# A 64-expert layer with three of four batches sorted, its indexed reads moved inside the causal attention

## The reference, cut to what matters

```python
# sub-layer 8 ("L2_ffn"): 64 experts, each token takes the best 8
scores = softmax(x @ gate_w.T)
topk_w, topk_ids = top_k(scores, 8);  topk_w /= topk_w.sum(-1) + 1e-20
h = silu(rows @ w_gate[e].T) * (rows @ w_up[e].T)      # 96 wide, per expert e
y = sum over the 8 of topk_w * (h @ w_down[e].T)
# sub-layer 9 ("L3_attn"): causal attention, 16 heads of 8, then a layer norm
att = where(causal, q @ k.T / sqrt(8), -inf);  y = layernorm(softmax(att) @ v @ Wo + bo)
```

## Time and profile before

| what | us |
|---|---|
| median of 3 runs | 1896.92 |
| lowest and highest of them | 1888.32, 1905.2 |
| the profiled execution | 1892.54 |
| its span, first to last instruction | 1890.8 |
| mean granted TensorE clock | 0.946 |

### The profile page before, as it was taken

How to read it: one execution, slowest core, us unless ns; L and a number is a source line. 1 busy time by engine, 2 the same in 40 slices (tenths; PEclk the granted TensorE clock), 3 DMA queues, 4 the chain that set the end, 5 groups by cost and what they waited for, 6 DMA issues and landing times. The chain is left out here.

```text
span 1890.8 us, 50187 instructions
## 1 busy us (share of the span) xinstructions
PE 1677.6 (89%) x19970; PEld 1202.2 (64%) x19970; DVE 1131.9 (60%) x2410; ACT 977.4 (52%) x2317; POOL 706.1 (37%) x947
## 2 busy tenths in 40 slices
PE   7883899775799999999999878899999999999885
PEld 4332899343457889989888753567996655454332
DVE  5534445559556777877776434676657866555334
ACT  4651444548586666666674435234553253445562
POOL 1103311305256777666775201473006621223101
PEclk9996999886699999999999989899999999999998
DMA  7401786000031000000000040523643200000100
GB/s 298 177 1 57 210 241 204 25 1 1 1 145 48 26 15 25 14 15 25 15 24 16 26 201 1 129 78 110 169 135 83 66 5 1 2 2 1 41 1 24
DMA packets 75929, 125.69 MB, mean 66 GB/s; under 512 B 10728, under 2 KB 55152, under 8 KB 74320
## 3 DMA queue, kind: packets, MB, share of 16 engines
q1 hardware_dynamic: 67696, 106.69, 17.5%
q0 software_dynamic: 6912, 15.61, 2.8%
q10 hardware_dynamic: 1088, 0.13, 0.0%
HBM read 83.73 MB, written 38.67 MB: 65 GB/s over the span
## 5 line engine op out<-in xcount | busy, mean ns | idle before, releaser
L2947 DVE SCALAR_TENSOR_TENSOR big<-bank,pack,big 128x256 f32<-128x256 f32 (+2 forms) x384 | 181.4, 474 | 40.6 <-ACT mask L2836 25.4
L2174 ACT ACTIVATE pack<-bank 128x512 f32<-128x512 f32 x96 | 57.5, 600 | 159.6 <-PE bank L834 93.8
L2643 PE MATMUL bank<-y,pack 128*128 128x262 f32 (+1 forms) x384 | 134.5, 435 | 5.5 <-DVE big L2947 5.1
L3375 ACT ACTIVATE pt<-bank 128x1024 f32<-128x1024 f32 (+3 forms) x128 | 84.2, 704 | 105.7 <-PE bank L3221 105.5
L3405 DVE TENSOR_REDUCE part<-bank 128x8 f32<-128x1024 f32 (+1 forms) x80 | 95.6, 1220 | 68.2 <-PE bank L3202 68.2
L2553 POOL TENSOR_TENSOR big<-big,mask 128x256 f32<-128x256 f32 (+1 forms) x128 | 93.7, 732 | 111.2 <-DVE big L2947 110.0
L2835 ACT ACTIVATE big<-bank,pack 128x256 f32<-128x256 f32 x192 | 91.1, 475 | 84.3 <-PE bank L2643 78.8
L1979 POOL DMA_INDIRECT pack<-results,where x64 | 67.0, 1047 | 151.2 <-PE bank L2049 137.6
L832 PE MATMUL bank<-yh,wl 128*128 128x512 f32 x192 | 113.3, 590 | 10.9 <-DVE a L2330 8.3
L2630 PEld LDWEIGHTS bank<-big 128*128 128x128 f32 x896 | 113.3, 193 | 7.1 <-issue 1.4
L2630 PE MATMUL bank<-big 128*128 128x128 f32 x896 | 116.2, 277 | 0.0
(11 more groups left out here) (672 smaller groups left out, 4396.7 us busy)
## 6 DMA issues: line engine op xcount, KB each, us to landing
big<-in_experts SPq DMA_DIRECT2D x46, 516.0 KB
big<-in_big SPq DMA_DIRECT2D x1, 9216.0 KB, 25.9
gate<-big SPq DMA_DIRECT2D x32, 256.0 KB
z<-gate SPq DMA_DIRECT2D x16, 512.0 KB
pack<-routing SPq DMA_DIRECT2D x60, 128.0 KB
wide_sorted<-big SPq DMA_DIRECT2D x5, 1472.0 KB, 13.1
pack<-in_pack SPq DMA_DIRECT2D x1, 5910.5 KB, 21.5
pack<-wide_sorted SPq DMA_DIRECT2D x16, 256.0 KB, 3.2
```

Source lines behind the costliest of these rows:

```text
L2643: nc.tensor.matmul(haloed(i)[:, :, 3 - halo:], k.w["L2_attn_qkv_w"][:, sl(m, P)], tokens, start=True, stop=True).then_inc(s["raw"], 1)
L2947: ins = nc.vector.scalar_tensor_tensor(out=d, in0=conv_in(i, back), scalar=weight(i, 3 - back), in1=d, op0=ALU.mult, op1=ALU.add)
L3375: nc.scalar.activation(dst, src, ACT.Exp, scale=-1.0).then_inc(s["weights"], 1)
```

## The change

Sub-layer 8 now has one dense batch (2) and three sorted ones (3, 0, 1), `WIDE_ORDER` = (2, 3, 0, 1):

- All 48 blocks of the one dense batch run ahead of the tiles; none run behind them. The table of router weights is half as wide; blocks below 3 are split by GpSimd.
- 96 indexed writes in place of 64; they no longer wait for down products. `locate`, `situate`, `code`, `put` work on 768 columns in place of 512. 159 tiles (80 pairs) in place of 127 (64 pairs).
- Behind the dense blocks, ahead of the tiles: batch 2 is added to x, its attention norm, q, k, v, per-head keys and the first 6 of its 20 looks.
- The indexed reads, the sums and the joins leave sub-layer 8. Sub-layer 9 takes the batches in `WIDE_ORDER`. It starts with the 14 remaining looks of batch 2 and 16 of 96 reads; the other 80 reads are dealt out over 36 units (`GATHERS`). ScalarE scales each read row (8 instructions on 128 x 128 for each of 12 tiles), and VectorE sums the 8 with one reduction.
- For each of the three sorted batches the following stands in the units of the batch before it: four tiles scaled and summed, `join`, norm, q, k, v, per-head keys, all 20 looks. The looks therefore come in the last three (batch 0 in the order) or five units.

In `layer6` the last token block's key transposes and their copies are left out, with the waits that this needs.

```diff
-WIDE_TILES = (2 * S * 8 + 64 * (P - 1)) // P
-WIDE_SPLIT, WIDE_POOLED, WIDE_MAP_AT = 24, 6, 13
+K8, WIDE_ORDER = 8, (2, 3, 0, 1)
+WIDE_ROWS = 3 * TB
+WIDE_TILES = (WIDE_ROWS * P * K8 + 64 * (P - 1)) // P
+WIDE_POOLED, WIDE_MAP_AT = 3, 13
...
-            for i in range(HALF):
+            for i in range(ROWS):
                 for c in range(K8):
-                    after(pool, s["down"], (i * K8 + c) * 2 // 3)
-                    nc.gpsimd.indirect_dma_start(out=rows_in, ...
+                    nc.gpsimd.indirect_dma_start(out=rows_in, ...
...
+            pe.wait_ge(s["done"], 1)
+            nc.tensor.matmul(first_xc, k.w["centre"], x[:, sl(DENSE)], start=True, stop=True).then_inc(s["first_centred"], 1)
...
+            for n in range(EARLY_LOOKS):
+                if n == 0:
+                    pe.wait_ge(s["k_out"], 1)
+                after(pe, s["most"], n - 2)
+                look_products(nc, k, late, 0, n, both(n)).then_inc(s["scores"], 1)
...
+            pe.wait_ge(s["v_out"], 1)
+            pe.wait_ge(s["most"], EARLY_LOOKS)
             pe.wait_ge(s["down_in"], 16)
             address(0)
             turn(0)
...
+    GROUPS, UNITS, KEEP, LAG = 4, 16, 4, 3
+    JOIN, QK, V, SHIFT = (9, 7, 7), (12, 10, 10), (13, 11, 11), (14, 13, 13, 13)
+    per_unit = [(0,) * 13 + (6, 7, 7)] + [(0,) * 11 + (4, 4, 4, 5, 3)] * 2
+    HEAD_GATHERS = 16
+    GATHERS = (2,) * 8 + (1,) * 5 + (5,) * 3 + (3, 2, 2, 2, 2, 2) + (1,) * 5 + (4,) * 5 + (2, 2, 1, 1)
...
+            def scale_rows(i):
+                act.wait_ge(s[f"got_{i % TB}"], 16 * K8 * (i // TB + 1))
+                for c in range(K8):
+                    row = found[:, sl(i % TB * K8 + c, P)]
+                    ins = nc.scalar.activation(row, row, ACT.Copy, scale=late.share[:, c * WIDE_ROWS + i:][:, 0:1])
+                ins.then_inc(s["rows_scaled"], 1)
...
+            def mix(i):
+                dve.wait_ge(s["rows_scaled"], i + 1)
+                parts = found[:, sl(i % TB, K8 * P)].rearrange("p (c e) -> p e c", c=K8)
+                nc.vector.tensor_reduce(mixed[:, sl(i % TB, P)], parts, AX.X, ALU.add).then_inc(s["mixed"], 1)
...
-                elif phase == KT:
+                elif phase == KT and u // B < TB - 1:
```

More of the change, by code:

```diff
@@ new lines, with look_products @@
+EARLY_LOOKS, EARLY_ROWS = 6, 2
+def look_products(nc, k, late, b, n, dst):
+    i, kind, key, w, js, gp = LOOKS[n]
+    if kind == 0:
+        for gl in range(2):
+            nc.tensor.matmul(dst[:, sl(gl)], k.ident_bf, late.later4[:, :], start=True, stop=False, skip_group_check=True)
+    for c, j in enumerate(js):
+        for gl in range(2):
+            rows = sl(2 * gp + gl, 32)
+            mm = nc.tensor.matmul(dst[:, gl * S + c * w:][:, 0:w], late.qj[b][rows, j * S + i * P:][:, 0:P], late.kd[b][rows, key:key + w],
+                                  start=kind != 0, stop=True, tile_position=(rows.start, 0), skip_group_check=True)
+    return mm
@@ L1866, in layer8 @@
[L1866 to L1872 removed]
+        whole, number, codes = sb("whole", MOST + 2, I32), sb("number", MOST + 2), sb("codes", K8)
@@ L1931, in _ @@
                 store(p)
-            for q in range(before, G // 4):
-                bring_rep(q)
         @block.gpsimd
@@ L2035, in unit @@
+                pe.wait_ge(s["mapped"], 2)
+                for i in range(2):
+                    mm = nc.tensor.matmul(mapped[0:1, sl(i, P)], expert[:, i:i + 1], k.ident, start=True, stop=True)
+                mm.then_inc(s["mapped_ps"], 1)
+            def unit(m):
                 if m < WIDE_POOLED:
@@ L2394, in _ @@
             strike(1)
-            mark()
-            order()
-            order_kept()
-            for m in range(WIDE_SPLIT):
-                dense(m)
-                if m == 1:
+            mark(1)
+            order(1)
+            for m in range(J):
+                scale(m)
+                hidden(m)
+                if m == 0:
+                    locate()
+                    situate()
+                    code()
+                    put()
+                if WIDE_POOLED <= m + 2 < J:
+                    split_low(m + 2)
+                if m == 2:
```

844 lines of the change are left out of this document (424 added, 420 removed).

## The result

| | before | after |
|---|---|---|
| time, us (median, lowest to highest, 4 runs each) | 1895.86 (1888.32 to 1905.2) | 2066.45 (2063.92 to 2069.39) |
| ratio, 95% interval | | 1.0898 [1.0847, 1.0949] |
| span of the profiled execution, us | 1890.8 | 2064.6 |
| forecast, us | | 1884 (1842 to 1912) |

The account below looks back on a forecast made before the run. TensorE was taken as the bound, busy for 89% of the span. -120.0 + 29.1 + 25.1 + 1.3 + 2.4 - 31.0 + 87.7 - 3.0 = -8.4 took 1892.5 to 1884 us, range 1842 to 1912.

Parts of the forecast that it names:

- Part 2: Way to the first tile: dense blocks at 2.27 us, then a serial chain; first tile at 1336.0, +29.1 us.
- rival C: Dense stage: router loads set the blocks' pace, dense half ends some 20 us later, time 1902; chance 0.13.
- The misread row: Dense stage: a VectorE gap was blamed on router loads behind the 3 MB down-weight load; 6 us taken after the change.
- The chain behind the dense stage: Batch 2 behind its dense blocks, from down product through norm, q, k and looks to the last maximum: 26.5 us.
- Part 3: Tiles: 16 more pairs at 1.57 us each cost +25.1; table load +1.3, last eviction and stage change +2.4.
- Part 4: Attention prologue: 52.0 us go, 14 looks with turn and shift take 21 us beside 16 indexed reads; -31.0.
- Part 5: The 64 attention units: 273.5 us instead of 185.8, paced by GpSimd, ScalarE and serial chains; +87.7.
- Rival B: Attention units: thinly used TensorE lets its clock drop, adding 30 us, time 1914; chance 0.15.
- the serial chain to the keys: Attention units: from `join` through add, norm, q, k and placing to the first look, some 15.3 us per sorted batch.
- Rival A: Attention units: slack and spread reads and copies hide half of 66.9 us; time 1850, 1817 if all hidden; chance 0.27.
- Parts 1 and 6: Second dense half goes, -120.0 us; sub-layer 6 loses 8 groups of key transposes, -3 us.

Follow-up runs that it names:

- experiment 3: Kernel before the change, with only the wait of its 64 indexed writes on the down products taken out: 1947.4 us.
- experiment 5: Changed kernel with a wait put back on the indexed writes, one block per two writes (write n waits for n/2 down products): 1956.1 us.
- Experiment 12: Kernel before the change, with the wait of indexed write n moved from 2n/3 down products to 6 + 5n/8: ratio 0.9988 [0.9962, 1.0014].
- experiment 4: Changed kernel with the 3 MB load of the down weights issued behind all router-row loads: 2063.2 us.
- experiment 1: Changed kernel with the dropped wait put back, two blocks per three writes (write n waits for 2n/3 down products, at most 48): 1980.7 us.
- experiment 6: Kernel of experiment 1 with two bf16 products of 512 columns added ahead of each weigh in units 0 to 12 of each batch: 2044.8 us.
- experiment 7: Kernel of experiment 1 without the 96 indexed reads and the waits on them; scaled copies and sums stay, on stale rows: 1970.4 us.
- experiment 8: Changed kernel, writes still without a wait on TensorE, with four short GpSimd fills behind each indexed write: 1991.5 us.
- experiment 9: Kernel of experiment 5 with added bf16 products in units 9 to 11, six ahead of the normalized rows' wait, twelve ahead of the keys': 1935.85 us.
- experiment 10: Changed kernel with each of the 96 indexed writes as a plain 64 KB transfer, ungated and without fills; attention reads stay indexed: 1942.3 us.
- experiment 11: Changed kernel with one wait for all 48 down products ahead of the first indexed write: 2042.1 us.

## Why the prediction was wrong

**Part 2, the way to the first tile, is the step that failed.** It priced the writes rightly (1.26 us each, 121 us; measured 1.28 and 123) and took the dense blocks beside them at 2.27 us. I listed "ungated writes" as a side note of rival C and gave the lost gate no price of its own, because in before the writes seemed to cost TensorE nothing. Apart from the small gap they cost nothing there because of the gate. The term was +29.1; it came out at +133.4. With a gate of one block per two writes the first tile product stands at 1347.6 instead of 1446.9: 99 of the 104 us over the forecast are the lost wait, shown from both sides by experiments 3 and 5. That the wait does it is shown; how it keeps TensorE's signals on time is open, as experiment 5 contradicts the theory of the unbroken row.

**The misread row.** The gap of before was read as router loads behind a 3 MB transfer. Experiment 12 took the gap away without touching a load, and experiment 4 moved the load without touching the loss. The row even said so: the releaser that it named was another tensor, and I overruled it with a story. Had I looked at what lies beside the gap (17 writes that the gate did not hold), the main loss was there to be read at a scale of 7 us. In the versions that let the blocks run beside the indexed writes (experiments 1 and 5 to 9) a router load does hold VectorE once, for 4.3 to 6.1 us, and the dense stage ends at 1307.9 to 1312.7 us, where I had 1309.5. So those 6 us came true, by a row that did not show them.

**The chain behind the dense stage** was forecast at 26.5 us and takes 31.6 (1408.7 to 1440.3), within its bounds.

**Part 3, the tiles.** 80 pairs from 1446.9 to 1572.9 are 1.575 us each. That looks like the 1.57 of the forecast, but the forecast's figure took in both ends of the stage. By the same borders the 64 pairs of before, from 1311.4 to 1407.7, are 1.505 each. So a pair has become dearer. Eight pairs take 1.84 to 1.94 us where before has 1.32 to 1.41, and TensorE's weight loads wait for VectorE as often (waits of 1460 to 1565 us below; in all the tiles of before the like wait is 0.2 us):

```profile
PEld bank L2125 <- DVE a L2400: 5.0, 8, 0.7
```

Of the 7.0 us over, 4.6 are the pairs (126.0 us against 96.3 + 25.1) and 2.4 the ends of the stage. Why VectorE is later there was not taken apart.

**Part 4, the prologue.** 21 us forecast, 35.2 measured. From the first read to the first cut it takes 38.4 us in the changed kernel and 38.2 and 38.1 in experiments 1 and 4, but 24.5 to 29.0 in experiments 5, 6 and 8 to 11, which have the same 16 reads (the forecast, to the first cut, was 24). Without the reads it is no shorter than in the faster of these: from the last tile product to the first cut experiment 7 takes 28.8 us, experiment 8 with its reads 28.6. The 16 head reads are indexed transfers without a wait on TensorE too, and late signals are in the changed kernel's trace: two maxima start 1.2 and 3.5 us after the modelled end of their look. That they make the difference is only argued; why it strikes in some executions alone stays open.

**Part 5, the units.** Term +87.7; it came out at +140.9. GpSimd's 3.3 us a unit was right (3.1). Rival B, the clock, was right in kind: the batches run at 0.69 to 0.81. It had 30 us; what the clock costs in all was not measured. In experiment 9 the looks behind the twelve products run at the upper level, and the unit in which they begin is 2 to 4 us shorter. But at 275.6 us for three batches it is still 40 over the 235.3 forecast. The units with the looks take 42.9, 47.8 and 45.5 us there, not 31.7, 35.9 and 35.9. How much of that is the serial chain to the keys, which I priced at 15.3 us, and how much is TensorE waiting for VectorE's maxima, was not taken apart. Rival A is out: nothing hid the units. The rule of the Trainium skill cited there ("TensorE: Matmul & The Clock Gate") held: nothing passed a waiting scaled copy on ScalarE, whose 2388 instructions start in the same order in the changed kernel and in experiments 1, 5, 8 and 11. Part 1 of the same page of the Trainium skill calls the throttled state the default; the trace of experiment 5 agrees, as its products behind the thin stretch start at 0.50.

**Parts 1 and 6.** The second dense half went as counted. The 3 us of sub-layer 6 do not show: the first Silu of sub-layer 8 (its table load) lies at 1182.6 to 1186.1 us in before and experiments 3 and 12, and at 1184.9 to 1195.0 in the eleven traces with the change. The tail is 126.1 us against 125.6.

**The balance of the idea.** Even with the writes gated, the attention holds it back. Experiment 5 against before: the first tile product comes 36.2 us later, the tiles take 29.6 us more, the second dense half and the long prologue give 141.4 back (from the last tile product to the first cut 174.1 against 32.7), and the units take 136.9 more. The sum is +61.3, of a span 63.4 longer. The dense half that was removed had been the cover of the reads and the sums, and the looks that filled before's units lost their place with it.

## What to carry to other kernels

A wait that seems to serve no dependence may be a throttle: before dropping one, find in the trace what it holds back and price the stage with that running free. Where GpSimd's indexed transfers run beside TensorE work, try a wait on TensorE's own progress in front of each, one that hardly ever holds when all goes well: here it held once, for under 1 us, and won 99 us. And work that was hidden in a thick stretch should be moved into a thin one only with the lower clock in the sum, for the thin products and for the first ones behind them.

## What the runs showed of the hardware

- Indexed writes of 64 KB from GpSimd, one each 1.28 us and with no wait on TensorE's progress in front of them, delay what other engines learn of TensorE's finished products by 10 to 18 us beyond the modelled ends, and let a dense block pass only each 22.4 us instead of 2.25. The delay builds up over some 50 us. The handovers between ScalarE and VectorE stayed prompt.
- With such a wait in front of each write nothing of it is left in experiment 5 (one each 1.34 us, held once), and nothing in experiment 8, with four fills behind each (one each 1.95 us). The lack of pauses is not the cause by itself. What the wait changes is open.
- Plain transfers of the same size from the same queue, one each 0.53 us at 215 GB/s, don't do it.
- Writes without a wait and with no dense blocks beside them are hardly faster: 96 took 121.1 us, against 122.8 us beside the stalled blocks.
- TensorE stayed at 0.50 of its clock for 15 us of nearly unbroken work behind a stretch with 2.45 of 5 us busy. Filling a stretch to 104 of 113 us left the mean at 0.71. Behind twelve products right ahead of them the looks ran at 1.00.
